# VectorE finishes each expert tile one turn later, and every buffer gets one place per tile of a pass

## What is computed

```
x  = layernorm(x)
gate_probs = softmax(x @ gate_w.T + gate_b)            # 10 gates, the last 2 are null experts
weights, selected = top_k(gate_probs, 2)
combine_w  = weights of the true experts among the two, normalised to sum 1
expert_out[t,e] = x[t] @ expert_w[e] + expert_b[e]     # 8 experts, 512 x 512
out[t]     = sum over e of combine_w[t,e] * expert_out[t,e]
x          = x + tanh(g_ffn) * out
```

## Time and profile before

| | us |
|---|---|
| median of 3 runs (lowest, highest) | 1402.09 (1396.83, 1402.58) |
| the profiled execution's own time | 1396.64 |
| its span, first to last instruction | 1394.8 |
| expert stage in it, first to last product | 972.5 to 1388.0 |

### The profile page before, as it was taken

One profiled execution on the slowest core, in us unless ns is written; L12 is line 12 of the kernel. 1 busy time (PEld: TensorE's weight loads), 2 busy tenths in 40 slices (PEclk: granted clock), 3 DMA queues, 4 the chain that ended last, 5 costly groups with the idle time before them and its releaser, 6 DMA issues. The chain is left out here.

```text
span 1394.8 us, 30166 instructions
## 1 busy us (share of the span) xinstructions
PE 1310.6 (94%) x7339; PEld 670.9 (48%) x7340; DVE 1105.5 (79%) x2797; ACT 752.0 (54%) x2724; POOL 694.3 (50%) x645
## 2 busy tenths in 40 slices
PE   7999999999999999999999999983988989999997
PEld 5434555555555555555555555541444444444443
DVE  5777889999999999999999999875666655666665
ACT  5656666566666656666665666643433333434332
POOL 1501232445445445545544644545666666666664
PEclk9899999999999999999999999996999999999999
DMA  8145888888977779877879877883454546676772
GB/s 307 48 160 154 181 197 189 178 194 231 214 179 188 187 176 244 210 178 180 195 180 245 199 187 182 168 182 95 130 143 139 151 131 197 214 237 212 230 232 99
DMA packets 413298, 256.17 MB, mean 184 GB/s; under 512 B 338979, under 2 KB 350307, under 8 KB 413077
## 3 DMA queue, kind: packets, MB, share of 16 engines
q1 hardware_dynamic: 385365, 180.89, 53.7%
q0 software_dynamic: 27840, 74.18, 16.9%
HBM read 111.61 MB, written 75.01 MB: 134 GB/s over the span
## 5 line engine op out<-in xcount | busy, mean ns | idle before, releaser
L1042 ACT ACTIVATE expd<-banks,less 128x77 f32<-128x77 f32 x1024 | 317.3, 328 | 176.1 <-DVE less L1149 174.9
L926 PE MATMUL banks<-arena,zT 128*128 (+1 forms) x2292 | 410.8, 337 | 0.9 <-PEq L162 0.9
L941 PE MATMUL banks<-u_sb,pT 128*128 128x512 f16 x1728 | 383.5, 379 | 2.0 <-DVE x_out L1174 1.7
L1898 PE MATMUL banks<-arena,expert_yT 128*128 x1440 | 333.7, 382 | 3.4 <-issue 2.1
L926 PEld LDWEIGHTS banks<-arena,zT 128*128 128x128 f16 x2292 | 219.0, 98 | 165.3 <-issue 1.4
L941 PEld LDWEIGHTS banks<-u_sb,pT 128*128 128x128 f16 x1728 | 168.9, 98 | 199.6 <-DVE x_out L1174 2.4
L1898 PEld LDWEIGHTS banks<-arena,expert_yT 128*128 128x128 f16 x1440 | 141.8, 99 | 151.0 <-issue 10.5
L1042 ACT ACTIVATION_READ_ACCUMULATOR expd<-banks,less 128x1 f32 x1024 | 213.7, 209 | 0.0
L1923 ACT CAST expert_yT<-banks 128x512 f16<-128x512 f32 x120 | 70.2, 585 | 222.0 <-PE banks L1885 102.9
L1619 POOL DMA_INDIRECT table<-payload,row_i x128 | 159.6, 1247 | 60.1 <-issue 35.9
L2011 DVE SCALAR_TENSOR_TENSOR result<-banks,slots,biased 128x512 f32<-128x512 f32 x120 | 90.1, 751 | 101.1 <-remote 53.9
(11 more groups left out here) (185 smaller groups left out, 1675.0 us busy)
## 6 DMA issues: line engine op xcount, KB each, us to landing
comb<-x_out SPq DMA_DIRECT2D x64, 512.0 KB, 3.2
x_ln<-in_x_dram SPq DMA_DIRECT2D x64, 256.0 KB
x_res<-in_x_dram SPq DMA_DIRECT2D x64, 256.0 KB
w_raw<-in_L_ffn_expert_w_dram SPq DMA_DIRECT2D x64, 128.0 KB, 2.3
u_dram<-u_stage SPq DMA_DIRECT2D x12, 512.0 KB, 2.8
u_sb<-u_dram SPq DMA_DIRECT2D x6, 1024.0 KB, 8.1
arena<-in_L_xattn_w_kv_dram SPq DMA_DIRECT2D x4, 1024.0 KB, 7.4
slots<-table SPq DMA_DIRECT2D x150, 2.0 KB
```

Of the source, the lines that this page charges most:

```text
L926: last = pe.matmul(scores[s][k][:, 0:n], zT[:, s, zp, t, :], m, start=(t == 0 and (zp, mp) == PRODUCTS[0]), stop=(t == DT - 1 and (zp, mp) ...
L941: last = pe.matmul(mix[:], pT[:, s, pp, k, :], u_sb[:, k, up, :], start=(k == 0 and (pp, up) == PRODUCTS[0]), stop=False)
L1042: last = act.activation(expd[:, s, h * KEYS:(h + 1) * KEYS], scores[s][k][:, at:at + KEYS], ACT.Exp, bias=less[:, s, h:h + 1], scale=1.0 / ...
L1898: last = pe.matmul(c.out_bank[s][:], yT[:, s, yp, t, :], w_of[:, bass.ds(e, 1), t, wp * D:(wp + 1) * D].rearrange("p a n -> p (a n)"), sta ...
```

## The change

VectorE's turn becomes `low_y` of tile j+1, `name_token` of tile j+5, `weigh_bias` of tile j, and then `name_out` and `finish` of tile j-1. GpSimd scatters tile j-2 in turn j. A gather waits for `biased_ready` of the tile that had its place, no longer for its result. `expert_y`, the fp16 halves and the products' banks have five places, one per tile of a pass (the halves now lie in free room behind the expert weights, the products use all five remaining PSUM banks, the last one also for the warm-up matmuls); `biased` and the transposes' banks keep three. The waits on these buffers become five turns long, also from choice 0 into choice 1, and ScalarE's waits between the choices go; VectorE's and GpSimd's stay. The kernel's loops run one more empty turn at the end.

```diff
-        y = sb("expert_y", [P, TURNS, D], F32)
+        y = sb("expert_y", [P, R, D], F32)
         biased = sb("biased", [P, TURNS, D], F32)
-        yT = sb("expert_yT", [P, TURNS, 2, DT, P], F16)
+        yT = spare_room[:, 0:R * 2 * D].rearrange("p (s l t q) -> p s l t q", s=R, l=2, t=DT)
-        out_banks = banks[TURNS:2 * TURNS]
+        out_banks = banks[TURNS:TURNS + R]
...
-            for s in range(R + 1):
+            for s in range(R + 2):
                 step(last, s, lambda n: s + n < R, last_experts)
...
# GpSimd, gathers
                 if later(j, R):
-                    pool.wait_ge(c.result_ready, 2 * (j - R) + 2)
+                    pool.wait_ge(c.biased_ready, j - R + 1)
# GpSimd, step
-                    if live(-1):
-                        _, place, j = at(r, s, -1)
+                    if live(-2):
+                        _, place, j = at(r, s, -2)
                         scatter(c, place, j)
# TensorE, multiply
-                if later(j, 2):
-                    pe.wait_ge(c.result_ready, 2 * (j - 1))
+                if later(j, R):
+                    pe.wait_ge(c.result_ready, 2 * (j - R + 1))
                 elif c.k == 1:
-                    pe.wait_ge(choices[0].result_ready, 2 * (first_tiles - 1 + j))
+                    pe.wait_ge(choices[0].result_ready, 2 * (first_tiles - R + 1 + j))
# ScalarE, high_y
-                act.wait_ge(c.yT_summed, j + 1)
-                if later(j, 2):
-                    act.wait_ge(c.expert_summed, j - 1)
-                act.copy(yT[:, s, 0], c.yT_bank[s][:]).then_inc(c.y_hi_ready, 1)
+                if later(j, R):
+                    act.wait_ge(c.expert_summed, j - R + 1)
+                elif c.k == 1:
+                    act.wait_ge(choices[0].expert_summed, first_tiles - R + 1 + j)
+                act.wait_ge(c.yT_summed, j + 1)
+                act.copy(yT[:, s, 0], c.yT_bank[buffer(s)][:]).then_inc(c.y_hi_ready, 1)
# ScalarE, between the choices
-                if c.k == 1:
-                    act.wait_ge(choices[0].yT_summed, tiles)
-                    act.wait_ge(choices[0].expert_summed, tiles)
-                    act.nop(nofuse=True)
# VectorE, step
                     if live(1):
-                        low_y(c, R * r + s + 1, buffer(s + 1))
-                    if live(0):
-                        j = R * r + s
-                        name_out(c, r, s, j, tiles)
-                        weigh_bias(c, r, s, j, pass_experts[s])
-                        finish(c, r, s, j)
+                        low_y(c, R * r + s + 1, (s + 1) % R)
                     named = R if c.k == 0 else EARLY
                     if live(R) and not (first_pass(r) and s + R < named):
                         name_token(c, *at(r, s, R))
+                    if live(0):
+                        weigh_bias(c, r, s, R * r + s, pass_experts[s])
+                    if live(-1):
+                        behind, place, j = at(r, s, -1)
+                        name_out(c, behind, place, j, tiles)
+                        finish(c, behind, place, j)
```

More of the change, by code:

```diff
@@ L1686, in __init__, with run_experts @@
         self.put = [sem(f"put{s}") for s in range(RING)]
[L1689 removed]
+def run_experts(nc, ident, ones16, w_parts, slots, expert_bias, bias_in, got_rings, comb, x_final, table, listing, banks, spare_room):
     R = RING
@@ L1722, in run_experts @@
         cleared = stack.enter_context(nc.semaphore("cleared"))
-        spare_bank = banks[2 * TURNS]
+        spare_bank = out_banks[R - 1]
         warmed = stack.enter_context(nc.semaphore("warmed"))
@@ L1884, in transpose_y @@
                 for t in range(DT):
-                    last = pe.transpose(c.yT_bank[s][:, t, :], y[:, s, t * P:(t + 1) * P], ident[:])
+                    last = pe.transpose(c.yT_bank[buffer(s)][:, t, :], y[:, s, t * P:(t + 1) * P], ident[:])
                 last.then_inc(c.yT_summed, 1)
@@ L1907, in step @@
                     if live(1):
-                        transpose_y(c, R * r + s + 1, buffer(s + 1))
+                        transpose_y(c, R * r + s + 1, (s + 1) % R)
                     if live(0):
-                        multiply(c, R * r + s, buffer(s), pass_experts[s], tiles)
+                        multiply(c, R * r + s, s, pass_experts[s], tiles)
                 if c.k == 1:
@@ L1917, in _, with high_y, normalize @@
         def _(act):
-            def high_y(c, j, s):
+            def high_y(c, j, s, first_tiles):
+                if later(j, R):
+                    act.wait_ge(c.expert_summed, j - R + 1)
+                elif c.k == 1:
+                    act.wait_ge(choices[0].expert_summed, first_tiles - R + 1 + j)
                 act.wait_ge(c.yT_summed, j + 1)
-                if later(j, 2):
-                    act.wait_ge(c.expert_summed, j - 1)
-                act.copy(yT[:, s, 0], c.yT_bank[s][:]).then_inc(c.y_hi_ready, 1)
-            def normalize(c, r, s, j):
+                act.copy(yT[:, s, 0], c.yT_bank[buffer(s)][:]).then_inc(c.y_hi_ready, 1)
+            def normalize(c, r, s, j, first_tiles):
                 act.wait_ge(c.got[s], 16 * r + 16)
-                if later(j, 2):
-                    act.wait_ge(c.yT_summed, j - 1)
+                if later(j, R):
+                    act.wait_ge(c.yT_summed, j - R + 1)
+                elif c.k == 1:
+                    act.wait_ge(choices[0].yT_summed, first_tiles - R + 1 + j)
                 act.nop(nofuse=True)
                 own = slots[:, c.k, bass.ds(j, 1), 2:4].rearrange("p a b -> p (a b)")
-                act.activation(y[:, buffer(s), :], c.x_got[:, s, :], ACT.Identity, bias=own[:, 0:1],
+                act.activation(y[:, s, :], c.x_got[:, s, :], ACT.Identity, bias=own[:, 0:1],
                                scale=own[:, 1:2]).then_inc(c.y_ready, 1)
@@ L1937, in _ @@
             clear(one_ring[:].rearrange("p s d -> p (s d)"), R * D)
+            tiles = None
             for c in choices:
@@ L1940, in step @@
                     if live(1):
-                        high_y(c, R * r + s + 1, buffer(s + 1))
+                        high_y(c, R * r + s + 1, (s + 1) % R, tiles)
                     if live(2):
-                        normalize(c, *at(r, s, 2))
+                        normalize(c, *at(r, s, 2), tiles)
                     if c.k == 0 and first_pass(r) and s >= 0:
                         clear(two_ring[:, s].rearrange("p l d -> p (l d)"), 2 * D)
-                if c.k == 1:
-                    act.wait_ge(choices[0].yT_summed, tiles)
-                    act.wait_ge(choices[0].expert_summed, tiles)
-                    act.nop(nofuse=True)
                 tiles = run(act, c, step, 2)
@@ L1972, in low_y @@
             def low_y(c, j, s):
+                if later(j, R):
+                    dve.wait_ge(c.expert_summed, j - R + 1)
                 dve.wait_ge(c.y_hi_ready, j + 1)
-                if later(j, 2):
-                    dve.wait_ge(c.expert_summed, j - 1)
-                dve.tensor_tensor(yT[:, s, 1], c.yT_bank[s][:], yT[:, s, 0], ALU.subtract).then_inc(c.y_lo_ready, 1)
+                dve.tensor_tensor(yT[:, s, 1], c.yT_bank[buffer(s)][:], yT[:, s, 0], ALU.subtract).then_inc(c.y_lo_ready, 1)
             def weigh_bias(c, r, s, j, e):
@@ L2010, in finish @@
                 dve.nop(nofuse=True)
-                dve.scalar_tensor_tensor(result[:, s, :], c.out_bank[buffer(s)][:], own, biased[:, buffer(s), :],
+                dve.scalar_tensor_tensor(result[:, s, :], c.out_bank[s][:], own, biased[:, buffer(s), :],
                                          ALU.mult, ALU.add).then_inc(c.result_ready, 1)
```

2 lines of the change are left out of this document (1 added, 1 removed).

## The result

Beside each other on one chip, the kernel before took 1396.8 us and the changed kernel 1407.3 us (medians of 20 runs each): ratio 1.0076, 95% interval 1.0062 to 1.0089. The change made the kernel slower by 10.6 us on that chip. The forecast was 1395, 7.2 us faster than a kernel before of 1402.1. That base was the median of three runs; over 20 runs it is 5.3 us lower, so what the forecast missed is better read from the differences: 7.2 us faster against 10.6 us slower.

A forecast was written before the change was run, and what follows sets the result against it. TensorE was taken to bound the kernel, losing time to waits in the expert stage, mostly ahead of transposes. Gains of 3.2 + 3 + 1 = 7.2 us from 1402.09 gave 1395 us, by the bounds 1388 to 1399; stated range 1375 to 1412.

The forecast's parts named there:

- What bounds the kernel: Expert stage: TensorE, 94% busy, loses 52 us to waits, 33.1 of them ahead of transposes; its completion signals arrive late.
- `finish` behind `low_y`: VectorE's turn in the expert stage: products stop waiting for `low_y`, 3.2 us gained; the transposes' wait stays untouched.
- Deeper buffers: Five places in the expert stage: `high_y` waits for the product of five tiles ago; costs and gains nothing by itself.
- Earlier gathers: GpSimd's gathers wait for `weigh_bias`, so choice 1's rows come sooner for `normalize`: 3 us gained, bounds 0.3 to 7.7.
- The passage: Between the choices: one DMA instruction out of the way of the last scatters, 1 us gained, bounds 0 and 2.67.
- The sum: Whole kernel: 3.2 + 3 + 1 = 7.2 us gained, bounds 3.5 and 13.6.
- Rival A: Expert stage: undoing the ring of waits between VectorE and GpSimd ends the late signals; 34 us off, 1368; chance 0.13.
- Rival B: Expert stage: what products gain is waited for at the next transposes, nothing comes off; 1401 to 1402 us; chance 0.2.
- Rival C: GpSimd's unbroken DMA run beside TensorE makes late signals more frequent; choice 1 above 3.41 us a tile, 1410 us; chance 0.2.

The follow-up runs named there:

- late chip: Chip or occasion with late TensorE signals; the kernel before took 1396.8 us where the change was timed, 1394.3 beside one experiment.
- quiet chip: Chip or occasion whose traces show no late signals; the kernel before took 1358 to 1361 us beside most experiments, the changed kernel 1353.8 against 1358.5.
- third chip: Kernel before 1386.7 us; changed kernel with choice 1's results written by plain transfers and ScalarE normalizing before its copy in choice 0: 1376.0.

## Why the prediction was wrong

*What bounds the kernel.* Right. The windows and waits had the late signals as what costs TensorE its time, and where there are none the kernel takes 38 us less.

*`finish` behind `low_y`, 3.2 us.* The waits ahead of products went, except at the start of choice 1, where one of 1.8 us stands for the earlier 0.4. The statement that it costs nothing else was too short: `finish` a turn later costs 21 us unless the gathers are freed from it at the same time.

*Deeper buffers, nothing.* Their nothing was argued from order alone, and I gave no thought to whom the old short waits held back. This was not tried by itself. On the late chip the early gathers carry 5.3 to 5.7 us of the 10.6, and what is left, some 5 us, belongs to the later `finish` and scatter, the buffers and the passage together; it is not divided.

*Earlier gathers, 3 us gained.* This is the step that failed. Its bounds were 0.3 to 7.7 us of gain, without a loss, although the row that it quoted, GpSimd's 2.79 us of waiting in the earlier trace rows, was the pause in which the late signal came out. It took the lateness of the signals as given, whatever GpSimd does. On the quiet chip the term's size holds: 1360.2 - 1356.8 = 3.4 us gained. On the late chip 5.3 us are lost. The mechanism as far as the traces go: the pair that GpSimd may now issue without waiting stands between the end of the transposes and the signal. The mean lateness goes from 1.92 to 2.35 us in about as many cases, and ScalarE's waits with it from 3.19 to 4.35 us. Why a transfer of GpSimd should hold a signal of TensorE back stays open.

*The passage, 1 us.* Its five turns had 10.3 us over 3.03 each before and 10.8 after. Nothing came.

*The sum.* The bounds 3.5 to 13.6 hold what a chip without late signals gives, 4.7 and 5.5 us. That is partly luck: the terms were worked out from waits that belong to the late chip. Where there are late signals, it misses a term of its own, and one more that I had left out: the price of the clock after a long stall. Outside the passage TensorE had never stood longer than 1.6 us before; now it does so for 2.4 us or more eight times, and five of these are followed by the lower clock, at 1.68 us each.

*Rival A* asked whether undoing the ring of waits ends the late signals. It doesn't on the late chip: 22 are left. The Trainium skill, page "TensorE: Matmul & The Clock Gate", section "The cost: per-tile semaphore tail", gives a tail of 25 ns, with 4.7 ns more for each tile and 26.3 for each increment; by estimate one increment is out in some 56 ns. The quiet chip's 0.09 us from the end of the transposes to the start of the copy agrees with a delay of that order, the late chip's 3.79 us does not.

*Rival B* had the transposes' wait take back what the products won; they took back more.

*Rival C* named the place, GpSimd's now unbroken run of transfers beside TensorE, and the point from which it decides, 3.41 us a tile in choice 1. It came to 3.47, and to 3.70 in choice 0. Its price was 1410; measured were 1407.3. That the price came so near is partly luck: C had the whole loss in choice 1, and 9.5 of the 14 us lie in choice 0. What I held against it, the ramp in choice 0's window, didn't bear on whether signals come later; that the late signals of the earlier trace rows came out in a pause of GpSimd did, and I gave it no weight.

## What to carry to other kernels

A pause in an engine's queue can be what keeps another engine's signals in time. Before taking a wait away, look in the trace at what happened right after it ended, and bound the cost on the side of a loss too. And where the trace shows waits for which it has no releaser, time the change on a second chip and at a second time: the same change took 0.3 to 0.4% off the time there and added 0.76% here.

## What the runs showed of the hardware

- On some occasions, but not on others (by chip or by time, see above), TensorE's completion signals reach ScalarE and VectorE up to 4 us late, while GpSimd issues indirect transfers one behind the other (about 1.03 us each, 0.31 apart); in the timeline above the signal came 1.07 us after the last one's end. The kernel before differs by 38 us between those occasions (1396 and 1359), all of it in the stage with these transfers in each turn. The traces with late signals also lack many records of semaphore updates. That GpSimd's series is the cause is supported by where in a series the late signals lie and by the third chip's choice 1, but not shown: no run on the late chip took the transfers away.
- Of eight stalls of TensorE of 2.4 us or more outside the passage, five were followed by 12 matmuls in 4.44 us (clock 0.62 in the one measured), three by 12 in 2.75; the longest of all, 2.73 us ahead of the transposes at 1195.04 us, is one of the three.
- A gather's record on GpSimd begins 0.79 us after the end of its own wait where GpSimd was idle (44 of 49 gathers in the changed kernel's first trace and all 32 on the quiet chip, within 0.01 us).
- An indirect scatter cost GpSimd about 1.0 to 1.5 us, a plain one of the same bytes 0.58 us; on the quiet chip this changed nothing in the total (0.9970 and 0.9971, against 0.9969 and 0.9961 with the indirect ones).
